# Graph network on one core: the count matrix built inside the three later attention passes, gathered pairs of rows stored from ScalarE's and SyncE's queues

## What is computed

```python
# L0: attention over edges (scores from el[src] + er[dst], softmax per dst, weighted sum of h[src])
# L1: sums by src of 128 edge features and node rows, then three linear layers with softplus
# L2: three times: h = x @ W; alpha = leaky_relu(al_s[src] + al_d[dst] + al_e)
#     coef = softmax of alpha over the edges of each dst; out[dst] = sum(h[src] * coef); batch norm
# L3: five times: agg = segment_sum(h[src], dst); two linear layers, three batch norms
```

## Time and profile before

| | us |
|---|---|
| median of 3 runs | 8978.68 (8977.43 to 8986.32) |
| the profiled execution | 8993.16 |
| its span | 8991.8 |
| PE, PEld busy | 5567.6, 4477.6 |
| DVE busy | 4739.3 |
| ACT busy | 4511.6 |
| POOL busy | 4381.9 |

### The profile page before, as it was taken

One profiled execution on the slowest core, in us unless ns is written; L12 is line 12 of the kernel. 1 busy time (PEld: TensorE's weight loads), 2 busy tenths in 40 slices (PEclk: granted clock), 3 DMA queues, 4 the chain that ended last, 5 costly groups with the idle time before them and its releaser, 6 DMA issues. The chain is left out here.

```text
span 8991.8 us, 135316 instructions
## 1 busy us (share of the span) xinstructions
PE 5567.6 (62%) x30230; PEld 4477.6 (50%) x30231; DVE 4739.3 (53%) x12204; ACT 4511.6 (50%) x8872; POOL 4381.9 (49%) x4415
## 2 busy tenths in 40 slices
PE   1621111756776886466665666656666498998986
PEld 1610001742225774355554555645555487776865
DVE  3820000559997877555554555555555645445455
ACT  1038886008996774444444444444444444444344
POOL 1877777737771000477774777747777300000000
PEclk8555555878888998787886888778888799999998
DMA  3433334855665441233332333323333286676764
GB/s 102 120 101 105 107 105 111 233 136 183 211 211 160 135 131 46 65 84 85 84 84 70 85 84 84 85 69 84 84 84 84 57 264 199 217 251 199 252 212 154
DMA packets 724312, 1173.04 MB, mean 130 GB/s; under 512 B 118807, under 2 KB 546470, under 8 KB 723608
## 3 DMA queue, kind: packets, MB, share of 16 engines
q1 hardware_dynamic: 366644, 612.04, 22.0%
q0 software_dynamic: 150784, 336.22, 15.6%
q10 hardware_dynamic: 206628, 221.92, 8.7%
HBM read 955.51 MB, written 216.73 MB: 130 GB/s over the span
## 5 line engine op out<-in xcount | busy, mean ns | idle before, releaser
L1204 POOL DMA_INDIRECT ring<-gat_rows,src_idx x2496 | 2417.8, 969 | 1004.4 <-issue 1001.3
L1324 PE MATMUL ps<-ring,xT_b 128*128 x8192 | 1410.3, 325 | 1236.1 <-ACT xT_b L1410 1230.7
L1324 PEld LDWEIGHTS ps<-ring,xT_b 128*128 128x128 f32 x8192 | 1219.0, 228 | 1448.8 <-issue 1446.9
L1402 ACT ACTIVATE xT_a<-xT_a,state 128x514 f32<-128x514 f32 x1024 | 740.1, 723 | 1824.0 <-SPq L1176 1293.5
L1814 PE MATMUL ps<-wide,features 128*128 128x504 f32 (+1 forms) x6370 | 1438.8, 384 | 18.2 <-DVE features L1714 16.2
L1814 PEld LDWEIGHTS ps<-wide,features 128*128 128x128 f32 x6370 | 1156.8, 189 | 252.3 <-DVE wide L1682 17.4
L1372 DVE CUSTOM_DVE_ANT_0 xT_a<-ps,mask,xT_a 128x512 f32<-128x512 f32 x1024 | 767.0, 749 | 607.5 <-PE ps L1315 488.8
L697 POOL DMA_INDIRECT by_src<-ring,state x832 | 803.4, 966 | 255.9 <-issue 253.0
L1054 POOL TENSOR_TENSOR x_nodes<-x_nodes,last_state 128x1280 f32<-128x1280 f32 x3 | 9.9, 3312 | 1792.2 <-SPq L227 1792.2
L1315 PE MATMUL ps<-ident,s_col 128*128 128x128 f32 x4096 | 747.0, 315 | 187.5 <-DVE s_col L1339 122.5
L1419 ACT ACTIVATE xT_b<-xT_a,neg 128x514 f32<-128x514 f32 x1024 | 741.6, 724 | 33.1
(11 more groups left out here) (383 smaller groups left out, 8761.4 us busy)
## 6 DMA issues: line engine op xcount, KB each, us to landing
xT_a<-adjacency SPq DMA_DIRECT2D x245, 756.0 KB
dl_all<-dloc_rows ACTq DMA_DIRECT2D x1052, 128.0 KB, 3.1
xT_b<-adjacency SPq DMA_DIRECT2D x150, 812.0 KB
xT_a<-adjacency SPq DMA_DIRECT2D x95, 812.0 KB
adjacency<-xT_b ACTq DMA_DIRECT2D x294, 252.0 KB
ring<-by_src SPq DMA_DIRECT2D x52, 1040.0 KB
ring<-gathered SPq DMA_DIRECT2D x208, 260.0 KB
ring<-in_edge_attr SPq DMA_DIRECT2D x103, 512.0 KB
```

The lines of the kernel that those rows point to most:

```text
L1204: pool.indirect_dma_start(ring[:, o:o + RC], None, table[:, :], bass.IndirectOffsetOnAxis(src_idx[:, t * W + u:t * W + u + 1], 0)).then_in ...
L1324: m = pe.matmul(bank(BO + v % 2, R), pw[v % 4][:, w * P:(w + 1) * P], ring[:, w * RC:][:, bass.ds(look(SLOT, u - 7), R)], start=w == 0, st ...
L1402: act.activation(um[u % 4], sm[u % 8], ACT.Identity, bias=S[:, ER:][:, bass.ds(look(BC, u), 1)]).then_inc(q["act_a"], 1)
```

## The change

- **The phase `adjacency` is gone.** The matrix is built in the three later attention passes, K = 256 steps each with STREAMS = 2 streams: 1536 steps for the 1472 before. Per step of a pass: VectorE makes the source matrices of both streams in one operation of 256 columns and two destination matrices of 504 (`make_nodes`); TensorE does four products of 504 columns (`add_counts`), for each stream the float16 window so far times the identity, or times zero where a new window begins, and the new column's product; ScalarE copies both windows to float16 (`evict_counts`) and issues two stores of 126 KB (`store_counts`), to the window's place when it is finished, else to a spare row. Scores are spread over two PSUM banks for four. TensorE loads 16 registers every eight steps, ScalarE four registers every two. Each pass loads its tables at the start; after the passes a window that both streams share is put together.
- **Gathering ahead**: tiles 0 to 13 in `positions`, 14 to 79 in `source_sums`, 80 to 95 in `adjacency_steps`. Pairs of tiles are stored by ScalarE's queue, in `source_sums` by SyncE's, in order between its loads. The other 112 tiles of the first pass are gathered straight into the ring during that pass, as slots are given back.
- **`positions` is written anew**: block numbers stay in memory on chip, edges on the partitions; per bin one compare over 832 columns, one-hot products that count, a scan over 832 columns, then per bin four products of 416 columns and a maximum over 832 columns.
- `adjacency_steps` loses one count and its rows and gets the tables of where each step's window is kept and stored, and writes the step columns (`of_steps`) to memory.

The core of the diff:

```diff
-FIRST = 32
-EARLY = 78
-TABLES = 90
+FIRST = 14
+EARLY = 80
+STORED = 96
-NH = 5
-HELD = 3
+NH = 3
+PAIR = 2
+STREAMS = 2
+PASSES = 3
+AK = STREAMS * PASSES * K
...
+            def rank_bins():
+                for b in range(BINS):
+                    for h in range(2):
...
+                        pe.matmul(to, earlier, hit[b][:, h * HT:(h + 1) * HT], start=True, stop=False)
+                        m = pe.matmul(to, choose[:, b:b + 1].to_broadcast([P, P]), pieces[:, h * HT:(h + 1) * HT],
+                                      start=False, stop=True)
+                    m.then_inc(q["masked"], 1)
+                for b in range(BINS):
+                    dve.wait_ge(q["masked"], b + 1)
...
+                    dve.tensor_tensor(two(best), two(best), halves(b % 4), ALU.max).then_inc(q["summed"], 1)
...
+        def keep_pair(eng, begin, n):
+            h = n % NH
+            eng.wait_ge(q[f"rows{h}"], 16 * PAIR * W * (n // NH + 1))
+            eng.dma_start(gathered[begin // PAIR + n, :, :], held[h]).then_inc(q[f"kept{h}"], 16)
...
         def gather_first_layer(begin, end):
-                if n >= HELD:
-                    keep(n - HELD)
...
         def stream_first_layer():
+            def watch(it, first=False, last=False, whole=True, whole_next=True):
...
+                        sp.wait_ge(q["product"], sp.snap(regs[g], min_val=1, max_val=K))
+                        later = g + SOON
+                        if whole if later < RT else whole_next:
+                            load(tile_of(it + later // RT, later % RT), later % RT)
+                        else:
+                            sp.sem_inc(q["room"], 1)
+                    landed(it, g, whole)
...
+            for t in range(STORED, T):
+                g = t % RT
+                pool.wait_ge(q["room"], t - STORED + 1)
+                for u in range(W):
+                    o = (g * W + u) * RC
+                    pool.indirect_dma_start(ring[:, o:o + RC], None, gat_rows[:, :], ...).then_inc(q[f"got{g}"], 16)
...
+            def make_nodes(n, u, have):
+                if have(2):
+                    dve.wait_ge(q["added"], n * STREAMS - STREAMS)
+                dve.tensor_tensor(node1[u % 4]..., node_row, src_steps..., ALU.is_equal)
+                for x in range(STREAMS):
+                    m = dve.tensor_scalar(node2[u % 2 * STREAMS + x], window_ids, dst_steps..., None, ALU.is_equal)
+                m.then_inc(q["eq"], 1)
...
+            def add_counts(n, u, have):
+                pe.wait_ge(q["eq"], n + 1)
+                if have(1):
+                    pe.wait_ge(q["out"], n * STREAMS)
+                if u % 8 == 0:
+                    keep_at[:] = rows_of(pe, 2 * U, 8 * STREAMS, keep_tab, n, P)
+                for x in range(STREAMS):
+                    pe.matmul(tile(x), carry[:, bass.ds(keep_at[u % 8 * STREAMS + x], P)],
+                              evicted[(u - 1) % 2 * STREAMS + x], start=True, stop=False)
+                    pe.matmul(tile(x), node1[u % 4][:, x * P:(x + 1) * P], node2[u % 2 * STREAMS + x],
+                              start=False, stop=True).then_inc(q["added"], 1)
...
+            def evict_counts(n, u, have):
+                for x in range(STREAMS):
+                    act.wait_ge(q["added"], n * STREAMS + x + 1)
+                    if have(2):
+                        act.wait_ge(q[f"st{u % 2 * STREAMS + x}"], (n - u) * 8 + u // 2 * 16)
+                    act.activation(evicted[u % 2 * STREAMS + x], tile(x), ACT.Copy).then_inc(q["out"], 1)
...
             def pe_body(n, u, have, look):
-                    if have(4):
-                        pe.wait_ge(q["masked"], n - 3)
+                    if have(wide_scores):
+                        pe.wait_ge(q["masked"], n + 1 - wide_scores)
...
+                if have(0) and not streamed:
+                    add_counts(n, u, have)
...
             def act_body(n, u, have, look):
+                if not streamed and u % 2 == 0 and (have(0) or have(1)):
+                    store_at[:] = rows_of(act, 2 * U, 2 * STREAMS, at_tab, n, DROP + NWIN - 1)
+                if have(1) and not streamed:
+                    store_counts(n - 1, (u - 1) % U, u)
+                if have(0) and not streamed:
+                    evict_counts(n, u, have)
...
-        def adjacency():
...
-        adjacency()
```

514 lines of the change are left out of this document (267 added, 247 removed).

## The result

The changed kernel takes **8446.4 us** (median of four runs, 8441.8 to 8453.3) against 8978.8 us (8977.4 to 8986.3): a ratio of 0.9406, interval 0.939 to 0.9422. It is 532 us faster; the forecast was 584. The profiled execution took 8444.4 us, its span is 8443.1, so the two spans differ by 548.7.

The account below looks back on a forecast made before the run. GpSimd's gathers were taken to bound the later passes, at 4.13 us a step. From the profiled 8993.2 us, terms summing to -584 and 14.5 off for the median gave 8395 us; range 8290 to 8640.

Parts of the forecast that it names:

- Count stage gone: The separate count matrix stage disappears, its gathers being made elsewhere: -703 us.
- steps: Stage of the count matrix's steps: 64 gathers for 48, and two writes of 786 KB with a landing: +23 us.
- Streamed pass: First pass: GpSimd idle for 281 us, then 570 of gathers and 24 to the end, 875 for 677: +198 us.
- rival 3: Later passes: each compare holds a gather for its whole length, 174 us a pass instead of 11; 8884 us; chance 4%.
- rival 2: Later passes: TensorE stays at 1.2 GHz, a step is 5.3 us; 9247 us, slower than before; chance 4%.
- Rival 1: Later passes: the other engines' step becomes the bound at about 4.5 us; 8617 us; chance 22%.
- 4.05 against 4.13: Later passes: ScalarE's estimated us a step against GpSimd's, so the gathers still cover the added work, with little to spare.
- landings still ahead of ScalarE's first activation: Later passes: sign for the forecast that ScalarE still waits for SyncE's landed tiles, with gathers 1.27 to 1.29 us apart.
- Three later passes: Each later pass gains 26 us, from slower gathers (11), steps that fall behind (9) and longer last steps (6): +78 us.
- Sums by source: 264 gathers for 184, and the last load waits for the last pair's store; GpSimd ends at about 370 us: +13 us.
- Ranks: Ranks of the edges, rewritten with compares, products and maxima, take 110 us, between 85 and 150: -199 us.
- Small edits: Joined step at the end is three chained transfers, the setup loses two: +6 us.

Follow-up runs that it names:

- experiment 2: Changed kernel, later passes written out: first without counting, 1078.8 us; second with one more ScalarE copy a step, grew by 121.7 us; third with two more.
- experiment 3: Changed kernel: first later pass makes the wide compares from two tensors, 1.167 us a gather; second has neither compares nor stores, 1102.6 us; third unchanged.
- experiment 1: Changed kernel: first later pass without the stores of the counts, 1125.1 us; second without the compares, 20 us shorter; third unchanged.
- experiment 8: The 6-of-16 kernel with the negated maximum of a step made by VectorE in place of ScalarE: 8293.6 us, 0.9221.
- 6-of-16 kernel: Changed kernel with stored tiles spread over the streamed pass, 6 of 16 ring slots loaded from them, 78 tiles ahead: 8239.3 us, 0.9171.

## Why the prediction was right, and where it was off

Right: the change is faster, the time is in the forecast's own range, and the big steps hold. That the sum is as close as 51 us is in part luck: its terms were off by 79 us one way and by 28 the other. *Count stage gone* and the *steps* together gave -675 for -680. *Streamed pass* +203 for +198, by its own three parts. The rivals did not come: the passes' clock rose to 0.91 (rival 2 needed it low), gathers were 0.995 us and not 1.15 (rival 3: a gather that started during a wide compare was held for 0.04 us on the mean and 0.17 at most, where the rival has a compare's whole 0.34). Rival 1 did not decide either, GpSimd waited for nothing, but experiment 2 shows that it was nearer than "4.05 against 4.13" reads: a step of the pass as it ran is 4.2, and 0.45 us on ScalarE came through whole. The sign that I named for the forecast, landings still ahead of ScalarE's first activation, failed in the sense that counts: it waits for one in 10 of 256 steps.

The 51 us between 8395 and 8446 are these terms:

- *Three later passes*, +78 forecast, +115 measured. The sizes were off, and of the gathers' part also the mechanism. Gathers: 21 us a pass for 11. The proportion that I took from the count stage by the length of compares has no meaning, since what counts is what runs at the moment when a gather starts, and whether it has two inputs in SBUF (experiment 3). The wide compares, which the forecast meant, cost 7.5 us a pass; the compare of the sources and the slope, which it did not think of, make the rest. End of the pass: 17 us for 15 (6 and 9); experiments 1 and 8 show that it is ScalarE's lag: the tail falls to 28 with the two stores' 0.85 us taken off ScalarE's sequencer, and to 30 with 0.24 us less on ScalarE. A step of 3.73 for 3.6 is in this: the issues of the stores were counted at 0.68 and took 0.85.
- *Sums by source*, +13 forecast, +29 measured. The step that fell short is "the last load waits for the last pair". The load does wait, and GpSimd ends at 387 for the 370 of the forecast, but this costs 8 us at most; 20 are there without it, and their cause is open.
- *Ranks*, -199 forecast, -221 measured. I added 30 us for products beside 80 us of VectorE; they were all covered. They were also priced too high: 0.435 us is the pitch of 504 columns, and these have 416. At the clock of 0.92 TensorE was busy for 64.2 us with all 300, where the forecast has 43 + 44 at the least.
- *Small edits*, +6 forecast, 0 measured. *Steps* and *streamed pass*: 5 us each.
- *From the profiled execution to the median*: 14.5 us were taken off, because the profiled execution of before was that much slower than its median. The profiled execution of after was 2 us faster than its median. Such an offset belongs to one execution and not to the kernel. That alone is 16 of the 51.

By sum: 37 + 16 - 22 - 6 + 10 + 16 = 51.

What the change left on the table was larger than any of these errors. Its +203 could be avoided by the order of the tiles, at 39 us in the steps stage, and the "GpSimd idle for 281" of the prediction had it in view; and 8239.3 us with the order changed is 207 us below the changed kernel.

## What to carry to other kernels

When work is moved from a stage that ends into a stage that has an idle engine, spread it over that stage: here stored and live tiles in turn cost 2 us of the pass, and stored tiles first cost 203. When two engines end up equally long per step, neither sum tells the time: count what is left after the last item of the leader, and expect that part of what one engine is relieved of comes back on the other (all of it in experiment 1, 8 of 17 us in experiment 8). To find what holds an asynchronous neighbour, sort its instructions by what was running when each started; the mean of a pass, or a later moment, mixes the causes. And try an edit of a shared loop body against every stage that uses it, not only the one it is meant for.

## What the runs showed of the hardware

An indirect gather of 0.944 us on GpSimd is stretched when it starts while VectorE runs certain operations, and not by an operation that starts later: by 0.16 us on the mean and 0.53 at most during an operation of 514 columns with two inputs in SBUF (410 gathers), by 0.04 and 0.17 during a plain compare of 504 columns of 16 bits with one (562), by up to 1.68 where several operations with two inputs follow without a gap (the gather of 2.63 us in experiment 3). A compare with one input that also sums never stretched it (240 gathers, 0.011 us at most), though it takes 0.73 us where the plain one takes 0.35. A load of registers cost ScalarE 0.31 us for 4 and 1.97 for 32, which is 0.08 and 0.06 a register.

One chip ran the kernel before 18% slower than the others and the 6-of-16 kernel 21% (9963.0 against 8239.3). Operations of VectorE, ScalarE and GpSimd were as long there; TensorE's were longer (the products with the gathered rows 322 ns for 298) at a granted clock of 0.78 for 0.84. The idle time between instructions is not spread evenly: between two of the sort's 832 scatters it is 0.305 us on the median on both chips, but 41 gaps of over 1 us add up to 244 us there, for one of 2.6 us elsewhere. What makes them is open. GpSimd waited for room there and hardly at all elsewhere, so what bounds a stage can differ from chip to chip, and kernels are to be compared on one.
